# Turning the normalised x by a DMA from ACT's queue instead of by TensorE, with scales spread and products added at two seams

## The reference, cut to what matters

```python
x = x + tanh(g_xattn) * attention(layernorm(x), ctx, ctx)   # 16 heads of 16, biases on q, k, v and out
x = x + tanh(g_ffn)   * ffn(layernorm(x))
def ffn(x):                                # act_qdq: scale = max|x| / 32767 over the WHOLE tensor, then round
    x = act_qdq(x)
    up, gate = act_qdq(x @ dq(w_up).T), act_qdq(x @ dq(w_gate).T)   # dq: 4 bits, one scale per 32 weights
    gate = act_qdq(gate * fixed_qdq_u16(sigmoid(gate)))
    return act_qdq(gate * up) @ dq(w_down).T
```

## Time and profile before

| what | value |
|---|---|
| median of 3 runs | 616.48 us |
| time of the profiled execution | 616.58 us |
| its span, first to last instruction | 614.7 us |
| mean granted TensorE clock | 0.981 |
| PE busy | 564.1 us, 92% |
| DVE busy | 493.8 us, 80% |
| ACT busy | 439.0 us, 71% |
| POOL busy | 207.5 us, 34% |

### The profile page before, as it was taken

The page is one execution under the profiler, slowest core; times in us unless marked ns, Lnnn a source line. Parts: engine busy times, 40 slices in busy tenths (PEclk is TensorE's granted clock), DMA queues, the critical chain, the costliest instruction groups (busy, mean ns, idle before and its releaser), DMA issues. The chain is left out here.

```text
span 614.7 us, 11698 instructions
## 1 busy us (share of the span) xinstructions
PE 564.1 (92%) x4315; PEld 339.9 (55%) x4315; DVE 493.8 (80%) x835; ACT 439.0 (71%) x632; POOL 207.5 (34%) x227
## 2 busy tenths in 40 slices
PE   2679999899999999999987899999999899949998
PEld 1345666566665666666445444444444344438887
DVE  5788889999999988998828599979988799954442
ACT  2237888678787777887766354549999998869860
POOL 4723347766666879755345000000000000010100
PEclk9889999999999999999999799999999999969999
DMA  6523344455544444433241000000000000023443
GB/s 192 133 87 116 102 127 130 120 144 134 144 132 138 125 132 127 119 81 106 66 116 53 2 1 1 0 1 1 1 1 0 1 0 1 1 69 104 138 138 103
DMA packets 42812, 48.98 MB, mean 80 GB/s; under 512 B 10436, under 2 KB 30532, under 8 KB 42756
## 3 DMA queue, kind: packets, MB, share of 16 engines
q1 hardware_dynamic: 40916, 43.38, 24.2%
q0 software_dynamic: 1408, 4.46, 2.6%
q10 hardware_dynamic: 432, 0.39, 0.3%
HBM read 24.32 MB, written 8.70 MB: 54 GB/s over the span
## 5 line engine op out<-in xcount | busy, mean ns | idle before, releaser
L872 DVE TENSOR_REDUCE negm<-s_ps 128x2 f32<-128x512 f32 x256 | 163.5, 682 | 25.2 <-PE s_ps L516 24.5
L695 ACT ACTIVATE pt<-st_ps 128x512 f32<-128x512 f32 x256 | 138.9, 596 | 54.8 <-PE st_ps L531 53.8
L1205 PE MATMUL pairs<-xq,wut 128*128 128x512 f16 x576 | 124.7, 379 | 2.7 <-ACT lnall L1357 1.6
L1205 PEld LDWEIGHTS pairs<-xq,wut 128*128 128x128 f16 x576 | 56.2, 98 | 71.1 <-issue 2.3
L516 PE MATMUL s_ps<-kst,qst 96*128 96x256 f16 x512 | 81.0, 274 | 11.0 <-DVE negm L872 7.6
L531 PE MATMUL st_ps<-qst,kst 97*128 97x512 f16 x256 | 76.5, 379 | 1.5 <-DMA qst<-mrow 0.9
L455 PE MATMUL pv_ps<-pt,vt 128*32 128x256 f32 x1024 | 68.5, 385 | 0.6 <-ACT pt L695 0.6
L1645 POOL PARTITION_ALL_REDUCE vmax<-vmax x5 | 1.8, 357 | 194.8 <-DVE vmax L1464 119.8
L516 PEld LDWEIGHTS s_ps<-kst,qst 96*128 96x128 f16 x512 | 46.0, 98 | 33.3 <-DVE negm L872 23.1
L1205 PE MATMUL pairs<-xq,wgt 128*128 128x512 f16 x276 | 60.5, 379 | 0.0
L1280 PE MATMUL pairs<-wdt,h 128*128 128x256 f16 x384 | 49.4, 281 | 8.4 <-ACT h L1393 8.4
(11 more groups left out here) (207 smaller groups left out, 1047.4 us busy)
## 6 DMA issues: line engine op xcount, KB each, us to landing
qst<-qk SPq DMA_DIRECT2D x96, 64.0 KB, 2.1
kst<-qk SPq DMA_DIRECT2D x45, 128.0 KB, 3.2
xt<-in_x SPq DMA_DIRECT2D x16, 256.0 KB, 4.3
ct<-in_ctx SPq DMA_DIRECT2D x16, 256.0 KB, 2.9
xr<-in_x SPq DMA_DIRECT2D x16, 256.0 KB, 3.9
out<-y SPq DMA_DIRECT2D x16, 256.0 KB, 3.8
lnall<-out POOLq DMA_DIRECT2D x8, 512.0 KB, 4.3
recb<-rec_dram SPq DMA_DIRECT2D x15, 256.0 KB
```

The lines of the kernel that those rows point to most:

```text
L695: nc.scalar.activation(pt[:, (j // 2) % 2, j % 2, kt], st_ps[u % 3][:], ACT.Exp, scale=1.0 / (WS * WS * HD ** 0.5)).then_inc(exp_done, 1)
L872: nc.vector.tensor_reduce(negm[:, b % 2, tt, lo:lo + 5:4], s_ps[tt][:], AX.X, ALU.max, negate=True).then_inc(max_done, 1)
L1205: mm = nc.tensor.matmul(ps[:, p, k, :], w[:, a, dt, f * P:(f + 1) * P], xq[:, b, c, dt, :], start=n == 0, stop=n == len(terms) - 1)
```

## The change

The turn leaves PE. In step 6 ACT casts xn to the high half and DVE makes the low half, both as x stands in rows, into xtok; in step 7 a DMA transpose on ACT's queue turns both halves into xtr, and q is projected from there. The k projection gets a wait on the low half of q (`before(g - 1, Q)` is b + 1 for batch b). POOL waits for xl_done where it waited for the turn. The block scales are taken apart and spread over steps of remainder 5 and 6 (two of them elsewhere), ln_max moves from step 6 to 7 and the clip from 4 to 5. Six products that nothing reads are put behind L623, and 32 behind the last up_again.

```diff
-    SCALES = (2, 34, 66)
+    SCALES = ((-3, -2, 5, 5, 6, 6), (21, 22, 29, 30, 37, 38), (54, 61, 62, 69, 70, 71))
-        xh = sb("xh", [P, 2, S], F16)
-        xl = sb("xl", [P, 2, S], F16)
+        xtok = sb("xtok", [P, 2, KT * D], F16)
+        xtr = sb("xtr", [P, 2, KT, 2, P], F16)
...
-                    pe.wait_ge(xl_done, b + 1)
+                    pe.wait_ge(x_turned, 16 * (b + 1))
                     pe.wait_ge(weights_low, 3)
-                    project(bank(g), "q", xh, xl, q_done)
+                    project(bank(g), "q", lambda k: xtr[:, 0, :, k, :], lambda k: xtr[:, 1, :, k, :], q_done)
                 if (b := batch(g, K)) is not None:
                     pe.wait_ge(top_done[1], before(g, TOP1))
-                    pe.wait_ge(xl_done, before(g, TURN))
+                    pe.wait_ge(top_done[0], before(g, TOP0))
+                    pe.wait_ge(ql_done, before(g - 1, Q))
...
-                if (b := batch(g, TURN)) is not None:      # PE
-                    pe.wait_ge(xn_ready, b + 1)
-                    for d in range(2):
-                        for tt in range(KT):
-                            mm = nc.tensor.transpose(to[:, d, tt * P:(tt + 1) * P], xn[:, tt, d * P:(d + 1) * P], ident[:])
...
+            for _ in range(6):
+                nc.tensor.matmul(s_ps[0][:].rearrange("p a b -> p (a b)"), wo2[:, 0, 0, 0:P],
+                                 wo2[:, 0].rearrange("p a b -> p (a b)"), start=True, stop=True)
...
-                if (b := batch(g, -17)) is not None:       # ACT
-                    act.wait_ge(xt_done, b + 1)
+                if (b := batch(g, TURN)) is not None:
+                    act.wait_ge(xn_ready, b + 1)
+                    act.wait_ge(x_turned, 16 * b)
+                    nc.scalar.copy(xtok[:, 0], xn[:].rearrange("p t d -> p (t d)")).then_inc(xh_done, 1)
+                if (b := batch(g, TURN + 1)) is not None:
+                    act.wait_ge(xl_done, b + 1)
                     act.wait_ge(q_done, b)
-                    nc.scalar.copy(xh[:], bank(PAIRS * b + TURN)[:]).then_inc(xh_done, 1)
+                    act.dma_start_transpose(xtr[:].rearrange("p i t u q -> p (i t u) q"),
+                                            xtok[:].rearrange("p i c -> p (i c)")).then_inc(x_turned, 16)
...
-                if (b := batch(g, 30)) is not None and b < LAST - 1:
+                if (b := batch(g, 31)) is not None and b < LAST - 1:
                     ln_max(b)
-                if (b := batch(g, -17)) is not None:       # DVE
+                if (b := batch(g, TURN)) is not None:
                     dve.wait_ge(xh_done, b + 1)
-                    nc.vector.tensor_tensor(xl[:], bank(PAIRS * b + TURN)[:], xh[:], ALU.subtract).then_inc(xl_done, 1)
+                    nc.vector.tensor_tensor(xtok[:, 1], xn[:].rearrange("p t d -> p (t d)"), xtok[:, 0], ALU.subtract
+                                            ).then_inc(xl_done, 1)
...
+                for i, steps in enumerate(SCALES):
+                    for p in range(PARTS):
+                        if g == steps[p]:
+                            part_scales(i, p)
+                    if g == steps[3]:
+                        scale_of_blocks(i)
+                    if g == steps[4]:
+                        inverse_of_blocks(i)
+                    if g == steps[5]:
+                        step_of_blocks(i)
+                for i, n in pieces_behind(g, 5):
...
-                    pool.wait_ge(xt_done, b)
+                    pool.wait_ge(xl_done, b)
...
+            def spare_products(bank, n):                   # feed_forward, PE
+                for _ in range(n):
+                    nc.tensor.matmul(bank, wgt[:, 0, 0, 0:P], wgt[:, 0, 0, 0:CW], start=True, stop=True)
...
             chunks(0, NC - 1, up_again)
+            spare_products(ps[:, 3, 1], 32)
```

More of the change, by code:

```diff
@@ L149, in attention, with two_halves @@
         recx = wi[:, 0:4 * S].bitcast(F32)
-        ahl, all_ = (xh, ch), (xl, cl)
+        def two_halves(i):
+            return xtr[:, i].rearrange("p t u q -> p (t u q)").rearrange("p (u s) -> p u s", u=2)
+        ahl, all_ = (two_halves(0), ch[:]), (two_halves(1), cl[:])
         ident_zeroed = sem("ident_zeroed")
@@ L193, in attention @@
         xn_ready = sem("xn_ready")
-        xt_done = sem("xt_done")
+        x_turned = sem("x_turned")
         xh_done = sem("xh_done")
@@ L420, in project @@
                 for e in range(2):
-                    mm = split_product(to[:, e, :], lambda k: wh[nm][:, k, e * P:(e + 1) * P],
-                                       lambda k: wl[nm][:, k, e * P:(e + 1) * P],
-                                       lambda k: xh_[:, k, :], lambda k: xl_[:, k, :])
+                    o = to[:, e, :] if nm == "k" else to[:, e, :].rearrange("p (t q) -> p t q", t=KT)
+                    mm = split_product(o, lambda k: wh[nm][:, k, e * P:(e + 1) * P],
+                                       lambda k: wl[nm][:, k, e * P:(e + 1) * P], xh_, xl_)
                 mm.then_inc(done, 1)
@@ L550, in _ @@
                     pe.wait_ge(ql_done, b)
-                    pe.wait_ge(xl_done, b + 1)
+                    pe.wait_ge(x_turned, 16 * (b + 1))
                     pe.wait_ge(weights_low, 3)
-                    project(bank(g), "q", xh, xl, q_done)
+                    project(bank(g), "q", lambda k: xtr[:, 0, :, k, :], lambda k: xtr[:, 1, :, k, :], q_done)
                 if (b := batch(g, K)) is not None:
                     pe.wait_ge(top_done[1], before(g, TOP1))
-                    pe.wait_ge(xl_done, before(g, TURN))
+                    pe.wait_ge(top_done[0], before(g, TOP0))
+                    pe.wait_ge(ql_done, before(g - 1, Q))
                     pe.wait_ge(kl_done, b)
                     pe.wait_ge(cl_done, b + 1)
-                    project(bank(g), "k", ch, cl, k_done)
+                    project(bank(g), "k", lambda k: ch[:, k, :], lambda k: cl[:, k, :], k_done)
                 if g == -12:
@@ L582, in _ @@
                     values(b, 3)
-                if (b := batch(g, TURN)) is not None:
-                    pe.wait_ge(top_done[0], before(g, TOP0))
-                    pe.wait_ge(ql_done, before(g, Q))
-                    pe.wait_ge(xl_done, b)
-                    pe.wait_ge(xn_ready, b + 1)
-                    to = bank(g)
-                    for d in range(2):
-                        for tt in range(KT):
-                            mm = nc.tensor.transpose(to[:, d, tt * P:(tt + 1) * P], xn[:, tt, d * P:(d + 1) * P], ident[:])
-                    mm.then_inc(xt_done, 1)
                 if (b := batch(g, TOP0)) is not None:
@@ L656, in high_last @@
                 act.wait_ge(v_done, NB)
-                nc.scalar.copy(ahl[v][:], at[:, 1 - v]).then_inc(ah_last, 1)
+                nc.scalar.copy(ahl[v], at[:, 1 - v]).then_inc(ah_last, 1)
             def high_of(b):
@@ L764, in part_scales, with scale_of_blocks, inverse_of_blocks @@
                                         apply_absolute_value=True).then_inc(blk_max, 1)
-            def block_scales(i):
+            def scale_of_blocks(i):
                 dve.wait_ge(blk_max, PARTS * (i + 1))
+                if i:
+                    dve.wait_ge(blk_scaled, 2 * i)
                 nc.vector.tensor_scalar(bs[:], bm[:], 1.0 / 7.0, 1e-12, ALU.mult, ALU.max).then_inc(blk_scaled, 1)
+            def inverse_of_blocks(i):
                 dve.wait_ge(blk_scaled, 2 * i + 1)
@@ L771, in block_scales, with step_of_blocks @@
                 nc.vector.reciprocal(bi[:], bs[:]).then_inc(blk_inv, 1)
+            def step_of_blocks(i):
+                dve.wait_ge(blk_scaled, 2 * i + 1)
                 dve.wait_ge(w_real, PARTS * i)
@@ L824, in low_last @@
                 dve.wait_ge(ah_last, v + 1)
-                nc.vector.tensor_tensor(all_[v][:], at[:, 1 - v], ahl[v][:], ALU.subtract).then_inc(al_last, 1)
+                nc.vector.tensor_tensor(all_[v], at[:, 1 - v], ahl[v], ALU.subtract).then_inc(al_last, 1)
             def low_of(b):
```

## The result

The changed kernel takes 620.62 us, the median of 6 runs, against 616.74 for the kernel before beside it: a ratio of 1.0058, 95% interval [1.0035, 1.0081]. It is slower, by 3.6 us. The forecast was 612.1 us, a gain; it was wrong in sign, and the time lies inside the range only because this had been stretched for the rivals. The profiled execution took 621.64 us (span 619.8) against 616.58 (614.7): 5.1 us more.

What follows compares the result with a forecast made beforehand. PE was taken to bound plain attention batches, with the y loop at nearly its pace. The terms -4.9 + 0 + 1.4 - 2.0 + 4.5 - 1.3 - 2.1 gave -4.4 us: 616.5 to 612.1 us, range 605 to 625.

Steps and rivals of the forecast that it cites:

- step 6: Start: the first DMA transpose delays q, then k and the first s; +4.5 us, bounds +2 and +6.5.
- step 1: Attention batches: the turn leaves PE and the y loop shortens by 0.35 us a batch for 14 batches; -4.9 us.
- Step 5: Batches with block scales: spreading the scales' pieces over more steps saves net -2.0 us, bounds -3.2 and 0.
- Step 2: ACT's queue: issuing the DMA transpose holds ACT 1.3 us, bounds 0.66 and 1.98, without stalling PE; 0 us.
- Step 3: Transpose landing in each batch: 3.4 to 4.3 us after issue, hidden before q is projected; 0 us.
- Rivals A and B: In every batch, ACT's issue exceeds 1.9 us (chance 0.20) or the transpose lands after over 4.5 us (0.10); 626 us each.
- rival B: Transpose lands after more than 4.5 us and PE stalls at q every batch; 626 us at 5.5, chance 0.10.
- Step 4: Attention batches: the k projection's new wait on q's low half costs 0.1 us a batch; +1.4 us.
- Step 7: First seam, end of attention: six unread products cost time but keep the clock up; net -1.3 us.
- rival C: Both seams: the unread products do not hold the clock; 617.5 us, chance 0.08.
- Step 8: Second seam, ahead of `down`: 32 unread products keep the clock at full speed; -2.1 us, bounds -2.9 and 0.

Runs made afterwards that it cites:

- e8: Changed kernel, but SP loads w_gate, bo, wo, bv and x of batches 2 and 3 only after the first transpose has landed: 617.79 us, ratio 1.0011.
- e1: Changed kernel, but batch 0 is turned on PE as in the kernel before: 616.89 us, ratio 0.9982.
- e14: Changed kernel with batch 0 turned on PE, timed a second time beside the unedited changed kernel: 615.66 us, ratio 0.9945.
- e3: Changed kernel, but the loads of w_gate and of x of batch 2 are issued some ten steps later: 622.42 us, ratio 1.0068.
- e11: Kernel before with the scales spread and the 32 products at the second seam, turn staying on PE: 612.38 us, ratio 0.9930.
- e9: Kernel before with the DMA turn from batch 1 on, k's new wait, and the maximum of normalised rows a step later: 622.48 us, ratio 1.0085.
- e12: Changed kernel with batch 0 turned on PE, k not waiting for q's low half, and without the six products: 612.99 us, ratio 0.9939.
- e15: Changed kernel with batch 0 turned on PE and k not waiting for q's low half, six products kept: 615.24 us, ratio 0.9957.
- e2: Changed kernel, but the k projection waits only for the low half of q of the batch before: 620.86 us, ratio 1.0057.
- e13: Changed kernel timed once more, unedited: 621.39 us, ratio 1.0054.

## Why the prediction was wrong, step by step

**Two steps failed: step 6, the start, and step 1, the turn itself.** The first is the larger miss in the trace, the second in the times.

**Step 6 (+4.5)** took a landing of "4.3 us" and bounded it by "6 us". It landed after 8.3 us, q started at 20.8 instead of 16.8, k at 25.6 instead of 21.1, and the first s came 9.0 us late in the trace. The row for 4.3 us was a median over 16 loads, nearly all issued in the steady part; the step itself noted that the queues were full of weights and still used it. The trace of before had a nearer row, the two loads of x issued at 12.11:

```profile
xt<-in_x SPq DMA_DIRECT2D x2, 256.0 KB, 5.8
```

The step also took the lower end of its own working, which gave 4.5 to 5.7. Its form was right (the chain runs ACT, DVE, k), but what the trace shows is twice the term; in time, undoing the turn of batch 0 was worth 4.7 and 6.7 us. e8 shows the loads as the reason, e1 and e14 that this one batch turned the sign of the result: with it undone the ratios are 0.9982 and 0.9945.

The sum also lacked what batches 1 to 3 lost in this trace, 1.9 us. A colder clock goes with it, and varies from run to run: of 20 to 60 us, 6.8 us were at half clock before, 17 in the changed kernel and in its repetition, 3.4 in e14. In the nine traces with 13.7 us or more, k of batch 3 was 1.4 to 3.5 us further behind the kernel before than k of batch 0; in e8 and e14 (6.8 and 3.4) by at most 0.2, but in e3 (6.8) by 2.3 and in e11 (10.2) by 2.7, so the clock is not shown to be all of it. A late start is not needed for it: e1 (16) and e9 (17) have it with batch 0 on PE, and e8, with the DMA, has it not. Whether it makes it more likely stays open.

**Step 1 (-4.9).** With the start undone too, the kernel stayed far from the forecast: what is missing is mainly the turn: e12 less e11 is +0.6 us [-2.0, +3.1] where -4.9 was forecast, and the ten gaps of the traces give 1.5 us, 0.15 a batch, the lower of step 1's bounds. The mechanism is there in plain batches, which are 0.4 us shorter. What failed is to count it for 14 batches as if all were plain: in e12's ten gaps PE was busy for 171.2 us where it was 175.7 in e11, 4.4 us less as priced, but the gaps were only 0.2 us shorter. So in e12 PE's freed time became waiting. Some of it goes with the slow issues: eight of the nine traces have one of 2.3 to 2.7 us just ahead of the second y, and from that y to the third take 17.8 to 18.2 us; e15 has 1.26 there and takes 17.6. What takes the rest was not separated.

**Step 5 (-2.0)** gave more, 3.7 us timed and 3.1 in the ten gaps. So steps 1, 4 and 5, forecast at -5.5 for batches 1 to 14, come to -5.0 from batch 3 to 15 in the trace, but by luck: the scales gave more than their term, k's wait cost nothing, and the turn gave less. Nor were the parts independent: the turn alone costs 11.9 us, since its low half stands behind DVE's maximum unless that moves, and since the batches with scales grow longer; the turn on top of e11 gives nothing.

**Step 2 (0)**: the issue was to take 1.3 us, a choice between wide bounds; the median is 1.30. **Step 3 (0)**: 4.0 us median for 4.3, and PE waited for the transpose once more after the start, for 1.0 us. Both miss the tail: an issue of 2.0 to 2.7 us one to four times in a run, one of which cost 5 us in e1. Rivals A and B had been priced for every batch. The estimate of 1.7 us from the Trainium skill (DMA: Bandwidth & Descriptors, sequencer time per DmaTranspose) lies above the ordinary issue of 1.25 to 1.4 us and below the slow ones: the measurement decides for 1.3. The 1 us that rival B gave for moving the 256 KB was 1.4 us in e8.

**Step 4 (+1.4)**: nothing, by e2 and e15. **Step 7 (-1.3)**: the clock fell all the same, as rival C had it for both seams; +0.2 in the trace, +0.5 us [-1.1, +2.1] timed. **Step 8 (-2.1)**: -2.2 in the traces; timed alone -0.6, not to be told from either 0 or 2.1; also the 0.7 us that was to stay is there, as a wait of 0.50 us at 557.97.

Set side by side in the trace, the 9.5 us between -4.4 and +5.1 are 5.8 of the start (10.3 at k for a term of 4.5), 1.9 of batches 1 to 3, 0.5 of the steady ones and 1.4 of the first seam. In time, the 8.0 us between -4.4 and +3.6 are mainly the turn (5.5), with the six products (1.8) and the start (0.2 to 2.2), less k's wait (1.4); about 1 us is left over, and each of these carries an interval of 1.6 to 2.8 us.

## What to carry to other kernels

A transfer put on the path of the first batch stands behind every load that the start has queued, even where the DMA engines look idle, so take its landing from that stretch, or keep the first item on the old way. Before work is moved to another engine, look at what stands directly ahead of the new producer in its own engine's order: here one 0.68 us reduction decided over 4 to 6 us. What an engine is relieved of in every batch is gained only in the batches in which nothing else is late. Time each part of a bundle alone: the part meant as a side step (the scales) carried nearly the whole gain, and the main one carried none that could be measured.

## What the runs showed of the hardware

- A DMA transpose of 256 KB, SBUF to SBUF, moves as 1056 packets under 512 B. Alone on the engines they ran in some 1.4 us (13.7 to 15.1 in e8), and it landed 3.2 us after its issue; ACT is held for 1.25 to 1.4 us of issuing in most cases.
- In 24 of 185 issues ACT was held for 1.9 to 2.7 us, each time with a 16 KB packet of instructions fetched during the issue.
- Behind 1.7 MB of plain loads of another queue its packets started 2.4 us after the issue ended (3.0 in e13, 3.3 in e2), though the DMA engines were busy for only 5% of the time from 13.8 to 15.0 us, and it landed after 8.3 us (8.3, 7.3).
- With six unread products (1.47 us) ahead of the first seam's hole of 1.5 us the clock still stood at half for 3.4 us in seven of ten traces; without them for 6.8 us in six of eight. 32 (7.07 us), which leave 1.47 us of the 8.4 us hole open, held it in all thirteen traces; without them it fell in all five.
